# 45 near taps for 49, far columns gathered in batches, and a chunk's work begun earlier in the stencil loop

## What is computed

```
xp = x @ in_w + in_b
x1 = silu(batch_norm(depthwise_conv3x3(x)))
offset = x1 @ off_w + off_b
mask = softmax((x1 @ mask_w + mask_b).reshape(N, H, W, G, P), -1)
samples = bilinear_sample(pad(xp), reference_point + tap + offset)
out = (samples * mask).sum(points) @ out_w + out_b
x = x + out
```

## Time and profile before

| | us |
|---|---|
| median of 3 runs | 698.0 |
| lowest, highest | 696.69, 699.97 |
| the profiled execution | 699.83 |
| its span, first to last instruction | 697.97 |
| PE busy | 593.9 |
| DVE busy | 583.2 |
| POOL busy | 318.7 |
| ACT busy | 227.5 |

### The profile page before, as it was taken

One profiled execution on the slowest core, in us unless ns is written; L12 is line 12 of the kernel. 1 busy time (PEld: TensorE's weight loads), 2 busy tenths in 40 slices (PEclk: granted clock), 3 DMA queues, 4 the chain that ended last, 5 costly groups with the idle time before them and its releaser, 6 DMA issues.

```text
span 698.0 us, 11520 instructions
## 1 busy us (share of the span) xinstructions
PE 593.9 (85%) x3630; PEld 444.2 (64%) x3630; DVE 583.2 (84%) x1068; ACT 227.5 (33%) x335; POOL 318.7 (46%) x332
## 2 busy tenths in 40 slices
PE   5988877879868968878878679889999999989995
PEld 4557656557556556556566557557777777776674
DVE  4589999999999999999999999816767776654877
ACT  6150502414314216107016000234454544424431
POOL 7507795897727795168278240201221211124322
PEclk9899999999999999999989899989999999999998
DMA  7096303003003006000000000000000000004211
GB/s 189 31 353 212 109 0 107 2 1 108 2 0 108 1 3 263 1 1 2 1 1 3 0 1 1 0 1 0 1 2 1 0 1 1 1 1 107 54 38 46
DMA packets 25724, 30.57 MB, mean 44 GB/s; under 512 B 5316, under 2 KB 17812, under 8 KB 25684
## 3 DMA queue, kind: packets, MB, share of 16 engines
q1 hardware_dynamic: 24094, 29.77, 13.1%
q0 software_dynamic: 896, 0.23, 0.4%
q10 hardware_dynamic: 694, 0.01, 0.1%
HBM read 24.94 MB, written 5.05 MB: 43 GB/s over the span
## 4 chain that ended last, share of the span: by engine, by line
PE 48%; DVE 25%; issue 12%; DVEq 2%; ACT 1%; DMA 0%; SPq 0%; POOL 0%; ACTq 0%; POOLq 0%
DVE prod L1481 11%; PE banks L851 11%; PE banks L967 8%; PE pair L947 8%; DVE outer L1418 4%; PE pair L1025 4%; DVE stencil L1424 4%; PE banks L957 4%; PE banks L1063 4%; PE pair L802 3%; PE pair L795 2%; PE banks L873 1%; DVEq L1481 1%; PE banks L939 1%; PE banks L918 1%
## 5 line engine op out<-in xcount | busy, mean ns | idle before, releaser
L851 PE MATMUL banks<-ident,prod 128*128 128x128 f32 x1568 | 222.9, 288 | 72.4 <-DVE prod L1481 70.1
L851 PEld LDWEIGHTS banks<-ident,prod 128*128 128x128 f32 x1568 | 184.0, 148 | 132.2 <-DVE prod L1481 108.2
L1481 DVE TENSOR_TENSOR prod<-shifted,stencil 128x1024 f32 (+1 forms) x224 | 238.2, 1086 | 5.3 <-PE banks L851 5.3
L1249 POOL TENSOR_TENSOR rstd_now<-mv_now,neg_half 128x2 f32<-128x2 f32 x32 | 23.0, 718 | 133.8 <-DVE mv_now L1533 133.8
L802 PE MATMUL pair<-xg,dw_diag 128*128 128x512 f32 x144 | 73.2, 609 | 0.3 <-DVE xg L1303 0.3
L1221 POOL CAST far_list_i<-far_list 1x8 int32<-1x8 f32 x8 | 33.7, 4217 | 74.9 <-DVE far_list L1467 47.0
L967 PEld LDWEIGHTS banks<-shifted 128*128 128x128 f32 x512 | 60.2, 192 | 8.1 <-issue 6.1
L967 PE MATMUL banks<-shifted 128*128 128x128 f32 x512 | 63.3, 277 | 2.3 <-ACT shifted L683 1.4
L947 PE MATMUL pair<-shifted 128*128 128x512 f32 x128 | 61.6, 604 | 0.7 <-ACT shifted L666 0.6
L1548 DVE TENSOR_REDUCE neg_max<-pair 128x1 f32<-128x1024 f32 x32 | 39.2, 1225 | 23.7 <-PE pair L947 22.6
L1418 DVE TENSOR_TENSOR outer<-hats 128x800 f32<-128x800 f32 x56 | 55.2, 986 | 0.5
(11 more groups left out here) (238 smaller groups left out, 895.0 us busy)
## 6 DMA issues: line engine op xcount, KB each, us to landing
shifted<-padded SPq DMA_DIRECT2D x42, 256.0 KB
shifted<-padded SPq DMA_DIRECT2D x14, 640.0 KB
res<-in_x_dram SPq DMA_DIRECT2D x4, 512.0 KB, 6.2
padded<-stage SPq DMA_DIRECT2D x4, 512.0 KB, 11.0
stage<-in_L_ffn_W_dram SPq DMA_DIRECT2D x16, 128.0 KB, 2.3
out_dram<-res SPq DMA_DIRECT2D x16, 128.0 KB, 1.8
padded<-stencil SPq DMA_DIRECT2D x2, 228.0 KB, 2.5
got<-padded,cell_now POOLq DMA_INDIRECT x28
```

The source lines that it names most:

```text
L851: mm = pe.matmul(acc_of(c, r), prod[:, d % PROD, r * G:(r + 1) * G, :].rearrange("p g c -> p (g c)"), ident[:, :], is_transpose=True, star ...
L1481: ins = ve.tensor_tensor(prod[:, dx:dx + n, :, :], shifted[:, dx:dx + n, bass.ds(((c % HALF) * ROWS + dy) * G, ROWS * G), :], stencil_of[: ...
```

## The change

- Taps: rows 0 and 6 of the 7 x 7 stencil lose their two end taps: 45 taps in 26 units, 19 pairs and 7 singles. Rows are taken in the order 1, 0, 2, 3, 6, 4, 5.
- Far flags: a point that would reach a dropped tap has to be gathered too. DVE's maximum of squares and flags go, and ACT's Square. ACT writes signs of offset - 2 and of -offset - 2 (`signs_of`), DVE two small instructions on the hats of the corner points (`corners`), and PE sums all of these over the partitions in six matrix products into one row.
- POOL: the list is worked in batches of four and three columns (`add_batch`). For each column that is not empty three copies (`take`), then eight steps for the whole batch (`cells`), four gathers for each such column, 18 steps for the batch (`corner_weights`), and four steps for each such column (`collect`).
- Order: the silu of chunk k + 2 is finished by DVE in turn k before the product of point 5, the list comes before point 4, the hats' buffer is given back before the last addition. PE starts the convolution at tap 4, counts at 18, adds the fix at 21, projects from 25, and puts the offsets of chunk k + 2 row by row at taps 32 to 38. ACT prepares ahead of clearing the stencil, and finishes silu ahead of the count.
- Logits are one instruction for four.

```diff
+ROW_ORDER = (1, 0, 2, 3, 6, 4, 5)
+TAP_AT = [(dy, dx) for dy in ROW_ORDER for dx in range(WIN) if not (dy in (0, WIN - 1) and dx in (0, WIN - 1))]
+NEAR = len(TAP_AT)
-AT_FAR, AT_CONV, AT_SAMPLES, AT_PROJECT = 18, 22, 35, 39
-AT_LIST = 5
-STENCIL_FILL = (0, 1, 1, 0, 1, 1, 0, 1, 1)
+AT_CONV, AT_FAR, AT_SAMPLES, AT_PROJECT, AT_OFFSETS = 4, 18, 21, 25, 32
+AT_LIST = 4
+AT_SILU = 5
+STENCIL_FILL = (0, 1, 1, 1, 2, 1, 1, 2, 1)
...
-                sc.activation(far_xy, raw[:, :, 0:2 * GP], ACT.Square).then_inc(square_done, 1)
...
+            def signs_of(k):
...
+                for i, sign in enumerate((1.0, -1.0)):
+                    last = sc.activation(signs[:, i, :, :], raw[:, :, 0:2 * GP], ACT.Sign,
+                                         bias=tap_bias[:, TAPS - 1:TAPS], scale=sign)
+                last.then_inc(signs_done, 1)
...
             def turn(j, conv_ahead):
+                prepare(j + 2)
                 clear_stencil(j)
-                prepare(j + 2)
-                count_out(j + 2)
+                signs_of(j + 2)
                 if conv_ahead:
                     silu(j + 3)
+                count_out(j + 2)
                 copy_out(j)
                 residual(j)
...
-                count = pair[1][:, 0:FAR_COLS]
-                pe.matmul(count, ones16[:, :], far[:, :], start=True, stop=False)
-                pe.matmul(count, ones[0:1, :], far_codes[:, :], start=False, stop=True).then_inc(far_mm, 1)
+                count = pair[1][0:1, 0:FAR_COLS]
+                by_corner = count.rearrange("p (g a b) -> p g a b", a=3, b=3)[:, :, 0:3:2, 0:3:2]
+                pe.matmul(count, ones[0:1, 0:1], far_codes[:, :], start=True, stop=False)
+                pe.matmul(by_corner, far_unit[:, :], at_corner[:, :, :, :], start=False, stop=False)
+                for i in range(4):
+                    mm = pe.matmul(count, far_unit[:, :], signs[:, i // 2, :, (i % 2) * GP:(i % 2 + 1) * GP],
+                                   start=False, stop=(i == 3))
...
+            def add_batch(k, j0, n):
+                codes = [gp.value_load(far_list_i[0:1, j0 + j:j0 + j + 1], min_val=0, max_val=MOST_CODE) for j in range(n)]
+                groups = [(code // GROUP_UNIT) % (ROWS * G) for code in codes]
+                for j in range(n):
+                    with gp.If(codes[j] > int(FAR_UNIT) - 1):
+                        take(k, (codes[j] // (G * GROUP_UNIT)) % ROWS * 3,
+                             (codes[j] % GROUP_UNIT).with_bounds(min_val=0, max_val=GP - 1), groups[j], j)
+                    gp.nop()
+                cells(n)
+                for j in range(n):
+                    with gp.If(codes[j] > int(FAR_UNIT) - 1):
+                        gather(j)
+                    gp.nop()
+                corner_weights(n)
+                for j in range(n):
+                    with gp.If(codes[j] > int(FAR_UNIT) - 1):
+                        collect(k, groups[j], j)
+                    gp.nop()
...
-                    with gp.Fori(0, LIST - 1) as j:
-                        code = gp.value_load(far_list_i[0:1, bass.ds(j, 1)], min_val=0, max_val=int(FAR_UNIT) * (P + 1) - 1)
-                        with gp.If(code > int(FAR_UNIT) - 1):
-                            add_point(k, (code // (G * GROUP_UNIT)) % ROWS * 3, (code % GROUP_UNIT).with_bounds(min_val=0, max_val=GP - 1),
-                                      (code // GROUP_UNIT) % (ROWS * G))
+                    for j0 in range(0, LIST - 1, BATCH):
+                        some = gp.value_load(far_list_i[0:1, j0:j0 + 1], min_val=0, max_val=MOST_CODE)
+                        with gp.If(some > int(FAR_UNIT) - 1):
+                            add_batch(k, j0, min(BATCH, LIST - 1 - j0))
...
-                own(ve.tensor_tensor(off_most[:, :].rearrange("p (r g) -> p r g", r=ROWS), far_xy[:, :, 0:GP],
-                                     far_xy[:, :, GP:], ALU.max))
...
-                own(ve.tensor_scalar(far_flags, off_most[:, :], float(REACH) ** 2, FAR_UNIT, ALU.is_gt, ALU.mult))
...
+            def corners(k):
...
+                for kx in range(2):
+                    x0, y0 = (2 * 3 * TAPS + TAPS - 1) * kx, 2 * 3 * TAPS * kx
+                    last = ve.scalar_tensor_tensor(at_corner[:, :, kx, :], at[:, 0, :, x0:x0 + 2 * TAPS + 1:2 * TAPS], 0.0,
+                                                   at[:, 1, :, y0:y0 + 3 * TAPS:2 * TAPS + TAPS - 1], ALU.is_le, ALU.is_lt)
...
-                    if q == list_at:
+                    if q == AT_LIST:
                         list_far(k)
+                    if q == AT_SILU and silu_next:
+                        finish_silu(k + 1)
```

More of the change, by code:

```diff
@@ L86 @@
 FAR_UNIT = 8192.0
+MOST_CODE = int(FAR_UNIT) * (5 * P + 1) - 1
+BATCH = 4
 PAIRS = B * H // ROWS // 2
@@ L94, in first_of, with freed_by @@
 def first_of(unit):
-    return unit // ROW_UNITS * WIN + unit % ROW_UNITS * 2
+    return UNIT_AT[unit][0]
+def freed_by(tap):
+    dx = TAP_AT[tap][1]
+    before = [t for t in range(tap - NEAR, tap) if TAP_AT[t % NEAR][1] == dx]
+    return before[-1] + 1
 class Own:
@@ L340, in hybrid_block_kernel @@
         fix_done = sem("fix_done")
-        gathered = sem("gathered")
+        gathered = [sem(f"gathered{j}") for j in range(BATCH)]
         point = sem("point")
@@ L785, in _, with offsets @@
                       start=True, stop=True).then_inc(bias_mm, 1)
-            def offsets(k):
-                pe.wait_ge(x1_done, k + 1)
-                pe.wait_ge(fold_done, 1)
-                if not isinstance(k, int) or k > 0:
-                    pe.wait_ge(square_done, k)
-                for r in range(ROWS):
+            def offsets(k, r0, r1):
+                if r0 == 0:
+                    pe.wait_ge(x1_done, k + 1)
+                    pe.wait_ge(fold_done, 1)
+                    if not isinstance(k, int) or k > 0:
+                        pe.wait_ge(signs_done, k)
+                for r in range(r0, r1):
                     o = pair[0][:, r * 256:r * 256 + 3 * GP]
@@ L1158, in _ @@
             own(gp.memset(fix[:, :, :, :], 0.0))
+            for v in (got_off, got_at):
+                own(gp.memset(v[:, :, :], 0.0))
+            own(gp.memset(got_mid[:, :, :], 0.0))
+            own(gp.memset(tap_c[:, :, :, :, :], 0.0))
             own.wait()
@@ L1185, in add_point, with gather @@
+            def gather(j):
                 for a in range(4):
                     gp.indirect_dma_start(
-                        out=got[:, a, :], out_offset=None, in_=table,
-                        in_offset=bass.IndirectOffsetOnAxis(ap=cell_now[:, a:a + 1], axis=0)
-                    ).then_inc(gathered, 16)
-                step(gp.tensor_tensor(frac[:, 0, :], pos[:, :], low[:, :], ALU.subtract), 7, False)
-                step(gp.tensor_tensor(tap_d[:, :], low[:, :], place_xy, ALU.subtract), 8, True)
@@ L1213, in add_point @@
                 to = fix[:, bass.ds(k, 1), bass.ds(group, 1), :].rearrange("p s a c -> p (s a c)")
-                step(gp.tensor_tensor(to, to, got_sum[:, 0, :], ALU.add), 22, True)
+                step(gp.tensor_tensor(to, to, got_sum[:, 0, :], ALU.add), 4, True)
                 gp.sem_clear(point)
+            def add_point(k, row3, col, group):
+                take(k, row3, col, group, 0)
+                cells(1)
+                gather(0)
+                corner_weights(1)
+                collect(k, group, 0)
@@ L1385, in weigh_hats @@
                 own(ve.tensor_tensor(hy, hy, weights_of(k).unsqueeze(3).to_broadcast([P, ROWS, GP, TAPS]), ALU.mult))
+            def corners(k):
+                own.wait()
+                if not isinstance(k, int) or k > 0:
+                    ve.wait_ge(far_mm, k)
+                    ve.sem_inc(dve_waited, 1)
+                at = hats[:, :, :, :].rearrange("p a (g q) t -> p a g (q t)", q=PTS)
+                for kx in range(2):
+                    x0, y0 = (2 * 3 * TAPS + TAPS - 1) * kx, 2 * 3 * TAPS * kx
+                    last = ve.scalar_tensor_tensor(at_corner[:, :, kx, :], at[:, 0, :, x0:x0 + 2 * TAPS + 1:2 * TAPS], 0.0,
+                                                   at[:, 1, :, y0:y0 + 3 * TAPS:2 * TAPS + TAPS - 1], ALU.is_le, ALU.is_lt)
+                last.then_inc(corners_done, 1)
             def project_out(q):
@@ L1515, in _ @@
             turn(0, True)
-            with ve.Fori(0, CHUNKS - 2) as j:
+            with ve.Fori(0, CHUNKS - 3) as j:
                 own.enter(j, per)
-                turn(j + 1, False)
-                own.leave(CHUNKS - 2)
+                turn(j + 1, True)
+                own.leave(CHUNKS - 3)
+            turn(CHUNKS - 2, False)
             products(CHUNKS - 1, BEGIN, UNITS)
```

239 lines of the change are left out of this document (139 added, 100 removed).

## The result

The changed kernel takes **760.1 us** (median of 4 runs, 759.69 to 760.64) against 697.5 us for the kernel before on the same chip (4 runs, 696.69 to 699.97): a ratio of 1.089, with a 95% interval from 1.086 to 1.092. The prediction was 703.5 us with a range of 684 to 720. Slower was right and so was POOL as the cause, but the size was not: +62.6 us and not +5.5.

A forecast was written before the change was run, and what follows sets the result against it. DVE was taken to set the convolution stage's pace, with POOL 2.7 us from holding it up. 699.83 - 27.5 for DVE + 33 for POOL's stalls = 705.3, at the median 703.5 us; range 684 to 720.

The forecast's parts named there:

- DVE's part, 27.5 us: DVE in the convolution stage: fewer taps, smaller flag and logits work, and no waits for PE save 27.5 us.
- Hats at 6.5 us into a turn: ACT at a turn's start: its moved work ends near 6.5 us, when DVE wants the hats, and costs nothing.
- The columns 1 3 2 2 0 1 2 0 and 44 gathers: POOL's gathered columns in each of the eight chunks, eleven in all, at four gathers each.
- Rival E: The change marks other columns than thought: with only the seven old ones gathered, 8 us of stall, 679 us; chance 0.04.
- The batch, 34 + 14.1 per column: POOL's work on a list: 34 us shared and 14.1 per real column; 48.1, 62.2, 76.4 us for one to three.
- A list pause of 6 us: POOL at DVE's MAX8: its next instruction takes longer, priced at 6 us a list while POOL is busy.
- POOL's jump back shows no pause: At POOL's loop head after chunks 2 and 3 the first instruction took 0.80 and 0.18 us, so no pause was priced.
- Stalls of 11.4, 8.9 and 8.9 us in turns 2 to 4, 33 in all: DVE standing at its list until POOL finishes chunks 1 to 3; total 33 us with a 4 us excess, bounds 15 to 50.
- rival A: The forecast itself: POOL late in turns 2, 3 and 4, 25 to 45 us of stall, 695.5 to 715.5 us; chance 0.57.
- The price of a stall in POOL's time: While DVE stands still, POOL's steps take 0.30 us each and a collection 1.95, against 0.94 and 4.5 when busy.
- Rival B: POOL keeps up, with chunk 1's batch ending before 180; 0 to 10 us of stall, 670.5 to 680.5 us; chance 0.15.
- Rival D: POOL's longer loop pauses 6 us once or twice more a chunk, adding 12 to 20 us: 715 to 725 us; chance 0.12.

The follow-up runs named there:

- e4_no_far: The changed kernel with POOL reading every list but adding no column, all gathers left out: 674.4 us, ratio 0.965 to the kernel before.
- e1_own_wait: The changed kernel with DVE waiting for the end of its own MAX8 right behind each list: 689.9 us, ratio 0.988 to the kernel before.
- e6_no_corners: e1_own_wait with the two corner instructions flagging nothing, so POOL gathers 7 columns with 28 gathers: 676.5 us, ratio 0.967 to the kernel before.

## Why the prediction was wrong, step by step

- **DVE's part, 27.5 us: right.** 27.4 us by the waits on the page, 28.8 us in e4_no_far. The undisturbed turns 0 and 5 took 46.30 and 46.33 us, 46.75 were forecast. (Turn 1, of which the prediction says 46 to 47.5, took 52.02: DVE stood 5.32 us there for POOL.) The wide products fell from 168 to 152, and the 0.57 us waits for PE are gone from all turns: PE's new order keeps up.
- **Hats at 6.5 us into a turn: right.** ACT's Relu of turn 1 ended at 119.35, 6.5 us after 112.85, and DVE weighed the hats at 119.45. ACT's moved work cost nothing.
- **The columns 1 3 2 2 0 1 2 0 and 44 gathers: right.** Rival E falls.
- **The batch, 34 + 14.1 per column: mis-sized, on the safe side.** With the holds gone (e1_own_wait) chunks of one, three and two columns took 40.4, 69.2 and 53.5 us from the cast to the last addition, where 48.1, 76.4 and 62.2 were forecast; some 3 us of the last ran while DVE stood. Of the 7 to 9 us, 2.7 are the head (6.0 us from the cast to the first take, not 8.7).
- **A list pause of 6 us: this step failed.** I had read 6.75 us twice in the earlier trace rows and added 6 us for each list while POOL is busy. It was not a price but the distance from MAX8 to DVE's next break, and the change took the breaks away. In its place came 20 to 23 us, and 32 us in the last chunk, where DVE has neither a break nor a one-input instruction. By e1_own_wait against the changed kernel, the holds cost 760.1 - 689.9 = 70.2 us, the added waits' own cost already taken off. The place could be seen: the zeros of `STENCIL_FILL` are in the diff, and the pause of 148.39 ends at 155.14, just where DVE's row has its 0.04 us of break. I had looked at what each fill costs on DVE, and not at what it does for POOL. There was a second sign in the earlier trace rows: the prediction says that POOL's jump back shows no pause, by the casts at 207.12 and 279.67, and passes over the one at 113.42, which took 6.45 us and ended at 119.87, just behind the 119.82 at which DVE began to stand 0.57 us for PE.
- **Stalls of 11.4, 8.9 and 8.9 us in turns 2 to 4, 33 in all: right in kind, wrong in size.** In turns 2 to 4 DVE stood 23.74, 14.41 and 14.42 us in front of MAX8, and also 5.32 in turn 1, 2.92 in turn 6 and 26.96 in the last chunk, places that I had called in time. Without the holds those of turns 2 to 4 were 0, 6.9 and 6.9: so the forecast of 8.9 for turns 3 and 4 was 2.0 too dear, and that of turn 2 should have been nothing, since POOL's batch was priced too high. The mechanism of rival A is real, and worth 13.8 us.
- **The price of a stall in POOL's time: right.** While DVE stood, POOL's steps followed each other in 0.2 to 0.4 us and gathers in 1.25.
- **Rival B** (POOL keeps up, 670.5 to 680.5 us) is what the changed kernel would have been without holds and without the four added columns: e6_no_corners, 676.5 us. **Rival D**, longer code that pauses: by the rule of the Trainium skill, "Runtime: NRT & Kernel Launch", section "Instruction fetch mechanics", POOL's loop of three times the length should stop at its jumps back. No pause of the 6 us that D priced is there: the casts at the loop's head take 0.18 us at 139.34, at 209.49 and at 270.35, with 2.47, 1.92 and 2.06 us of idle time ahead of them. Whether a shorter fetch hides in that idle time, these traces don't show. D's numbers, 715 to 725, lay nearest to the 760.1, but by luck: it added more pauses of 6 us, and what happened is that each grew.

The sum with the measured terms: 698.0 - 27.4 for DVE, + 13.8 for POOL's work and + 74.4 for the holds (88.2 less 13.8) is 758.8. It closes by the way in which the 27.4 was taken; with the 28.8 and 70.2 us of the experiments it comes to 753.2, so the terms are known to about 6 us; the cost of the added wait lies in that gap. The range failed for one reason: its bounds of 15 to 50 us were made by varying a number (the pause) within what rows of before showed, and nothing asked what made that number.

The Trainium skill, "SBUF — State Buffer", section "Who interferes with whom", says that VectorE and GpSimd share one port pair as an exclusive lock, that a DVE instruction with two SBUF inputs contends with a GpSimd instruction that reads SBUF, that reductions never do, and that the loser waits for the whole instruction of the other. The traces agree for the most part on who lets POOL through: most held instructions end about 0.12 us after the start of DVE's row maximum (164.99 against 164.87), though the cast of e4_no_far's turn 0 stayed held over two reductions. They do not agree on one instruction as the length of the wait: here it lasts over 21 to 32 instructions of DVE in a row, and an instruction that issues a gather is held too (23.10 us at 90.66).

## What to carry to other kernels

If POOL works beside a DVE that never rests, look for POOL instructions whose time is far above that of their like, and see what DVE does where they start and where they end: a pause of 6 us may be a distance and not a price. Behind a MAX8 give DVE a break, by a dependent instruction with nothing between or by a wait for itself; here a break of 0.14 us saved 70 us, though turns without a stall grew by 0.4 to 1.1 us. And when filling the last gaps of the busiest engine, ask who lived in those gaps, above all in a short edit of a table.
